# Moving two groups of attention products and the turning of c between steps, in a layer of attention and experts

## The reference

```python
xn = _layernorm(x, axis=-1)
x = x + attention(xn, Wq, Wk, Wv, Wo) + experts(xn, gate_w, expert_w, expert_b)
```

## Time and profile before

| | |
|---|---|
| median of 3 runs | 976.4 us (975.77 to 978.81) |
| the profiled execution's own time | 978.25 us |
| its span | 976.5 us |
| TensorE (PE) busy | 911.8 us |
| VectorE (DVE) busy | 734.4 us, 75% |
| POOL busy | 545.3 us, 56% |
| ScalarE (ACT) busy | 434.7 us, 45% |
| mean granted clock of TensorE | 0.986 |

### The profile page before, as it was taken

How to read it: one execution, slowest core, us unless ns; L and a number is a source line. 1 busy time by engine, 2 the same in 40 slices (tenths; PEclk the granted TensorE clock), 3 DMA queues, 4 the chain that set the end, 5 groups by cost and what they waited for, 6 DMA issues and landing times.

```text
span 976.5 us, 18753 instructions
## 1 busy us (share of the span) xinstructions
PE 911.8 (93%) x6589; PEld 453.6 (46%) x6589; DVE 734.4 (75%) x1328; ACT 434.7 (45%) x711; POOL 545.3 (56%) x553
## 2 busy tenths in 40 slices
PE   2888898989999999989999999998999999999897
PEld 1344344444454544545555555554454444544343
DVE  7888989887989899954444444466878887788893
ACT  5357867757755443432211111123443444434442
POOL 1544677576585446663333333228777777777651
PEclk9999999999999999999999999999999999999999
DMA  6365688798787443396655555556555574466441
GB/s 245 108 227 185 169 280 289 216 318 298 196 269 286 149 159 124 118 338 199 209 175 173 173 173 173 173 184 184 164 186 177 179 228 152 145 187 184 149 131 55
DMA packets 107963, 188.63 MB, mean 193 GB/s; under 512 B 11872, under 2 KB 65248, under 8 KB 102624
## 3 DMA queue, kind: packets, MB, share of 16 engines
q1 hardware_dynamic: 97072, 152.03, 46.8%
q0 software_dynamic: 10800, 35.40, 12.7%
HBM read 117.13 MB, written 70.25 MB: 192 GB/s over the span
## 4 chain that ended last, share of the span: by engine, by line
PE 68%; DVE 11%; DMA 7%; ACT 7%; issue 4%; POOL 2%; SPq 1%; another core or an unknown queue 0%; ACTq 0%; DVEq 0%
PE psum L985 19%; PE psum L1070 12%; PE psum L1094 6%; PE psum L1033 6%; PE psum L1020 5%; PE psum L1036 5%; PE psum L1002 5%; PE psum L1079 4%; PE psum L962 3%; DVE top L1573 3%; ACT pT L783 3%; DMA c_rows<-c_turn 2%; DMA w_rows<-w_hl 2%; PE psum L1004 2%; ACT x_in L716 1%
## 5 line engine op out<-in xcount | busy, mean ns | idle before, releaser
L783 ACT ACTIVATE pT<-psum,factors 128x512 f32<-128x512 f32 (+1 forms) x352 | 219.0, 641 | 247.4 <-PE psum L1020 227.4
L1573 DVE TENSOR_REDUCE top<-psum 128x1 f32<-128x384 f32 (+3 forms) x352 | 210.2, 636 | 26.6 <-PE psum L1004 25.8
L1070 PE MATMUL psum<-xT,w_att 128*128 128x512 f16 x768 | 197.6, 383 | 7.6 <-DVE xT L1524 5.0
L985 PE MATMUL psum<-w_exp,x_gT 128*128 x852 | 195.3, 379 | 0.7 <-DVE x_gT L1529 0.6
L1020 PE MATMUL psum<-q_stack,k_stack 98*128 98x256 f16 (+3 forms) x512 | 128.3, 303 | 16.7 <-ACT pT L783 13.0
L613 POOL DMA_INDIRECT x_g<-xn_rows,tok_of x71 | 67.1, 945 | 131.9 <-PE psum L962 129.3
L1002 PE MATMUL psum<-k_stack,q_stack 96*128 96x384 f16 (+3 forms) x512 | 126.8, 301 | 12.6 <-DVE top L1573 9.6
L1529 DVE TENSOR_TENSOR x_gT<-psum,x_gT 128x512 f16<-128x512 f32 x71 | 49.0, 692 | 103.8 <-ACT x_gT L807 83.3
L985 PEld LDWEIGHTS psum<-w_exp,x_gT 128*128 128x128 f16 x852 | 83.4, 98 | 85.8 <-issue 1.2
L807 ACT ACTIVATE x_gT<-psum 128x512 f16<-128x512 f32 x71 | 42.3, 597 | 169.9 <-PE psum L962 167.3
L597 POOL TENSOR_SCALAR_AFFINE_SELECT pT<-pT 128x512 f32<-128x512 f32 x128 | 98.4, 780 | 20.9 <-ACT pT L783 20.9
(11 more groups left out here) (176 smaller groups left out, 1276.7 us busy)
## 6 DMA issues: line engine op xcount, KB each, us to landing
y_rows<-y_sb SPq DMA_DIRECT2D x71, 256.0 KB
w_in<-w_all SPq DMA_DIRECT2D x12, 1024.0 KB, 12.5
q_stack<-qk_rows SPq DMA_DIRECT2D x96, 128.0 KB
k_stack<-qk_rows SPq DMA_DIRECT2D x96, 128.0 KB
x_in<-x SPq DMA_DIRECT2D x8, 1024.0 KB, 11.1
qk_rows<-q_hl SPq DMA_DIRECT2D x32, 256.0 KB
qk_rows<-k_hl SPq DMA_DIRECT2D x32, 256.0 KB
xn_rows<-x_in SPq DMA_DIRECT2D x8, 1024.0 KB, 5.4
```

Of the source, the lines that this page charges most:

```text
L783: act.activation(p_of(j, h, heads), banks[BANK_T + (NT_ * n + k) % 2][:, 0:W], ACT.Exp, scale=factors[:, 0:1]).then_inc(exp_done, 1)
L985: now = pe.matmul(banks[s % 4], x_gT[s % 4][:, xp * C + c, :], w_exp[:, bass.ds(e, 1), wp, c, :].rearrange("p e d -> p (e d)"), start=n == ...
L1070: now = pe.matmul(bank, w_att[:, what, wp, c, g * P:(g + 1) * P], xT[b % 2][:, xp * C + c, :], start=at_pass == 0, stop=at_pass == 3 * C - 1)
L1573: return dve.tensor_reduce(out=top[:, h:h + heads, i], in_=banks[BANK_S + k % 2][:, 0:heads * W].rearrange("p (h t) -> p h t", h=heads), a ...
```

## The change

Four edits:

- TensorE: groups 0 and 1 of the products of steps 0 to 14 leave the end of their step. They stand in the next step, behind the first half of `project_qk(0, ...)` and ahead of scores units 2 and 3. Step 15 keeps its groups at its own end.
- TensorE: c is turned behind shifted unit 10 in steps 0 to 14 too, and in step 15 behind its products.
- ScalarE: c is copied behind exponentials 9, and with that behind the key copy; in step 15 behind exponentials 10.
- POOL: in step 15 the gather for expert tile 1 is issued right behind that for tile 0, ahead of `low_o(14)`, `rope(0, 18)` and `mask(15, 0)`.

```diff
--- before.py
+++ after.py
@@ -644,6 +644,7 @@
                     pool.wait_ge(tok_done, 1)
                     pool.wait_ge(xn_stored, 16 * B)
                     gather_x(0)
+                    gather_x(1)
                 if N1 < n < N - 1:
                     pool.wait_ge(pv_done, J * n)
                     gather_y(late_tiles(n + 1)[0])
@@ -652,8 +653,6 @@
                 if n + 3 < N:
                     rope(0, n + 3)
                 mask(n, 0)
-                if n == N1 - 1:
-                    gather_x(1)
                 if n + 3 < N:
                     low_qk(0, n + 3)
                 if n in (CHOOSE + 2, CHOOSE + 3):
@@ -851,14 +850,14 @@
                 if n + G < N:
                     take_v(n + G, BANK_QV)
                 exps(n, 8)
-                if n < N1:
-                    copy_c(n + 1)
                 if n + 3 < N:
                     high_qk(1, n + 3)
                 exps(n, 9)
-                if N1 <= n < N - 1:
+                if n < N - 1 and n != N1 - 1:
                     copy_c(n + 1)
                 exps(n, 10)
+                if n == N1 - 1:
+                    copy_c(n + 1)
                 if n in TURN_AT:
                     for k in range(C):
                         high_x(TURN_AT[n], k)
@@ -1122,6 +1121,9 @@
                         pe.wait_ge(sum_done, outs_till(n))
                     xT_ready((n + 3) // G)
                     project_qk(0, n + 3, 0, 6)
+                if 0 < n < N1:
+                    times_v(n - 1, 0)
+                    times_v(n - 1, 1)
                 if nxt:
                     scores(n + 1, 2)
                     scores(n + 1, 3)
@@ -1224,18 +1226,16 @@
                     if n == G:
                         pe.wait_ge(w_lo_done, 4)
                     project_out(wo[0], BANK_KO, 0, 4)
-                if n < N1:
-                    turn_c(n + 1)
                 shifted_scores(n, 9)
                 if wo:
                     project_out(wo[0], BANK_KO, 4, 8)
                 shifted_scores(n, 10)
-                if n < N1:
+                if n == N1 - 1:
                     times_v(n, 0)
                     times_v(n, 1)
-                elif nxt:
+                if nxt:
                     turn_c(n + 1)
-                else:
+                elif not nxt:
                     times_v_last(0, 1, 2)
                 if wo:
                     project_out(wo[0], BANK_KO, 8, 12)
```

## The result

The changed kernel takes 987.56 us (median of 4 runs, 984.28 to 989.13) against 977.01 us (975.77 to 978.81) for the kernel before in the same comparison: a ratio of 1.012, with a 95% interval of 1.0096 to 1.0144. On the 976.4 us of before that is +11.7 us (9.4 to 14.1). The forecast was 984.3 us, +7.9 us: the right direction, from the right place, but too small, and outside the interval.

A forecast was written before the change was run, and what follows sets the result against it. TensorE, busy 93% of the span, bounds the kernel. Terms 0.45 + 1.7 + 4.5 + 2.95 - 3.35 = +6.25 us, plus 1.6 for the clock, give +7.9: 984.3 us, range 980.0 to 988.5.

The forecast's parts named there:

- Step 13, the wait: End of step 13: scores unit 1 waits 4.5 us for c's copy behind the key copy, net +4.5 us.
- Step 13, the clock: Behind step 13's stall: a stretch of TensorE at the lower clock, +1.2 us.
- Step 11: End of step 11: TensorE reaches the ranks early and waits for VectorE's `chosen`, net +1.7 us.
- (c): Rival: c's loads late in steps 5 and 8, +3.6, and lower clock after step 11, +1.2: 989.1 us; 10%.
- Step 14: After step 14: scores unit 1 waits for c behind the key copy, net +2.95 us, plus 0.4 for the clock.
- Steps 0 to 10 and 12, and c's loads: Late c stalls scores unit 1 after steps 1 to 3, only step 2 paying, +0.45 us; c's later stores and loads 0.
- Step 15: Step 15: no wait for c ahead of unit 9, first expert product at 429.2 instead of 432.56, -3.35 us.
- The second gather: Step 15: issuing it earlier leaves POOL's chain ahead of c 1 us shorter, cover only, 0.
- (a): Rival: POOL not held, key copies of steps 13 and 14 4.5 us earlier, both stalls gone: 975.2 us; 6%.
- (b): Rival: VectorE fed 3.14 us sooner, waits for its maxima, 9.6 us, shrink: 974.7 us if all went; 6%.
- (d): Rival: stalls partly made up by step 2's lower-clock stretch going and VectorE's waits in step 14: 981.1 us; 16%.

The follow-up runs named there:

- after_spread_later: Changed kernel with VectorE's last spread of step 13, spread_low(0, 0), moved into step 14; 987.22 us, ratio 1.0102.
- products_only: Kernel before with only the products of steps 0 to 14 moved into the next step, c and step 15 as before; 984.64 us, ratio 1.0084.
- only_0_10_12: Kernel before with the change to products and c in steps 0 to 10 and 12 alone; 977.34 us, ratio 1.001.
- gather_only: Kernel before with only the gather of expert tile 1 moved up in step 15; 980.18 us, ratio 1.0044.
- turn15_only: Kernel before with only the turning and copy of c in step 15 moved behind the products; 976.49 us, ratio 1.0004.
- after_again: The changed kernel measured and profiled once more, with no edit; 988.37 us, ratio 1.0115.
- keep_11_13_14: Changed kernel with products and c of steps 11, 13 and 14 at their old places; 979.75 us, ratio 1.0044.
- step15_only: Kernel before with the change's edits of step 15 alone, c turned behind the products and second gather moved up; 977.02 us, ratio 1.0003.
- step15_gathers: Kernel before with the step 15 edits, plus the gathers of the fifth and sixth expert tiles ahead of low_o(15); 977.14 us, ratio 1.0002.

## Why the prediction was right in direction and short in size

The wait, the places and the direction were right. What failed are three terms of the sum, each short by 1.3 to 1.6 us: the clock behind step 13's wait (1.2 us forecast, 2.8 measured), the clock behind step 11's wait (nothing forecast, some 1.3 measured in four profiles of five) and step 15's gain (-3.35 us forecast to the end, -1.8 and -2.1 in the two profiles). The first two are sizes; in the third the path was wrong, because the gain was not followed into the experts.

- **Step 13, the wait: right.** 4.5 us at scores unit 1, released by ScalarE's copy of c, was forecast and 4.50 us is what the row shows. The copy followed the key copy by 1.35 us (1.36 forecast), and the chain behind it is shown by `after_spread_later`. What I had overlooked is the second lock, the bank that waits for VectorE's sum, worth 3.0 us by itself. It changed no number of the changed kernel, since it ends sooner. But it was wrong to think that the place of c alone would decide: `products_only` loses 4.5 us in this step with c where it was.
- **Step 13, the clock: the term that was mis-sized.** I added 1.2 us for one stretch. Two came, 6.8 us, in which TensorE was busy 5.89 us at half the clock; at full clock that would be half as long, so by this estimate they cost up to 2.9 us. The segment grew by 7.27 us, 2.8 more than the wait, where wait and clock together were forecast at 5.7. The Trainium skill (TensorE: Matmul & The Clock Gate, on the clock gate) has it that idleness throttles the array and activity releases it, and this case's trace agrees: the granted clock was 1.00 while TensorE stood still from 381.0 to 384.4, and 0.50 behind.
- **Step 11: right in the wait, and a clock term put at nothing.** 1.56 us of wait, +1.5 us net in the first profile (1.7 forecast). I gave it no clock, and no reason for that; it stood only in rival (c). In four profiles of five a stretch at the lower clock follows and makes it +2.8 to +3.1.
- **Step 14: right.** 2.95 us and 0.4 for the clock forecast, +3.11 measured, by way of two waits of 1.26 and 1.51 us; there is no stretch at the lower clock behind them.
- **Steps 0 to 10 and 12, and c's loads: right.** Step 1 and step 2 have a wait of 0.31 us each at scores unit 1, where I had 0.45 with step 2 alone to pay; `only_0_10_12` at 1.001 shows that no more comes of it. A later store of c costs nothing: TensorE's waits for its load are 0.9 and 0.8 us in the two profiles of the changed kernel and 2.3 in that of before, which fits the 0 that I took.
- **Step 15: right in the segment, wrong in the total. This is the step of the reasoning that failed.** -3.35 us forecast, -3.42 measured, but I carried it to the end as a gain. In the two profiles of the changed kernel the experts give back 1.66 and 1.33 us of it; with step 15 alone they give back 3.27, and the total is the same as before (1.0003). I had looked at TensorE alone there. A hint lay in my own rows, though at another place: the DMA engines at a share of 1.06 and 0.99 around a stretch at the lower clock. At the end of step 15 of the kernel before their share is 1.00 from 420 to 425 and 1.10 from 425 to 430. I had not asked what the experts' first transfers would do if TensorE came sooner.
- **The second gather: wrong.** "Cover only: 0" was refuted by `gather_only`: it takes 2.3 us out of the wait ahead of unit 9 (2.74 to 0.44). And `turn15_only` gains only 1.8 us in the segment without it. The -3.35 us had taken it as given that the second tile is there when TensorE turns it, and laid the whole gain to the turning of c; that the segment came out at -3.42 is in part luck.

In sum, segments of `after_again` less what was forecast: step 13 +1.6, step 11 +1.3, step 15 with the experts +1.3, step 14 -0.2, and step 2's 0.45, which did not come. On the 7.9 us of the prediction that gives 11.4; measured were 11.7. That the two are so near is luck: other segments differ by 1 to 2 us from profile to profile, and the whole span of `after_again` is 10.3 us above that of before.

Of the rivals, (a) and (b) did not come: the key copies of steps 13 and 14 are as late as before, and VectorE's maxima cost 7.9 us instead of 9.6, 1.7 us and not all. (c) had the clock behind step 11 right, and c's loads wrong. (d) had parts made up. VectorE's wait in step 14 is 1.49 us before and after. The stretch at the lower clock of step 2 did go, and segment 2 is 1.05 us shorter, but one came in step 1 (segment 1 +0.96); `turn15_only`, which changes neither step, has the same pair, so it is scatter and no gain.

What stays open: why `gather_only` and `keep_11_13_14` end 4.3 us above the kernel before while `step15_only`, which contains the first, ends level. Their profiles show the lower clock at 442.1 and at 440.9, which `step15_only` does not have; by estimate from its 3.4 us that is up to 1.7. They also have 6.8 us at the lower clock in step 17, behind two waits of 1.5 to 1.8 us each, where `step15_only` has no lower clock: step 17 takes 27.1 and 26.8 us against 23.5. But the kernel before has such a step 17 as well (25.9 us), and one profile of each can't show how often it comes; that of `step15_only` is of an execution of 973.20 us, 3.8 below its median. And what delays the normalisation in `step15_gathers` stays open.

## What to carry to other kernels

Work that stands between a late result and the one who needs it is cover, even if it has nothing to do with either. Before it is moved away, list every semaphore behind it and the time at which each is given, not just that of the part that moves with it: here two locks lay behind the same products, and the three steps out of fifteen where VectorE had extra work paid for all of them. And a gain ahead of a stretch that lives on transfers is a gain only if those transfers land sooner too.

## What the runs showed of the hardware

- The lower clock lasted 3.4 us in most places where it came, but 6.8 us behind the wait of 4.50 us (384.4 to 391.2), and 6.8 us from 400.0 behind that of 3.69 us (`after_spread_later`). Waits as short as 1.56 to 1.73 us, with 0.30 to 0.36 us of idle some 2 us ahead of them, were followed by a stretch of 3.4 us in four profiles of five, the same code showing both. Behind the wait of 2.74 to 2.76 us for c in step 15 it lasted 3.4 us in four profiles and 6.8 in two. So the same wait had no fixed price in clock from one profile to the next.
- POOL's float32 addition of 128x512 takes 1.26 us alone and 3.19 us beside VectorE's float16 spread, and the other way round a VectorE operation of 0.42 us took 2.64 us and ended 0.05 us behind the second of two POOL operations. The Trainium skill (SBUF — State Buffer, on who interferes with whom) says that a VectorE instruction with two inputs in SBUF and a GpSimd instruction that reads SBUF contend for a shared port pair, and that it is taken as an exclusive lock for a whole instruction, so that the loser blocks. The first pair of rows agrees: POOL's addition ends 1.12 us after the spread (383.86 against 382.74). The second agrees in that VectorE is blocked, but not in how long: it began 0.21 us ahead of POOL's first operation and was still held over two of them. No run isolates the lock.
